# Layer 0 of a four-layer transformer stack: one program of sixteen half-batch rounds of four heads, in place of setup, two attentions and a feed-forward block

## The reference

```python
def cross_attention(q_in, kv_in, ...):           # H = 16 heads of K = 128
    qh = (q_in @ wq + bq).reshape(b, q_len, H, K)
    kh = (kv_in @ wk + bk).reshape(b, t, H, K)
    vh = (kv_in @ wv + bv).reshape(b, t, H, K)
    kh = concat([kh, bias_k]); vh = concat([vh, bias_v])      # a 257th key and value
    weights = softmax(einsum('bqhk,bthk->bhqt', qh, kh) / sqrt(K))
    return einsum('bhqt,bthk->bqhk', weights, vh).reshape(b, q_len, H * K) @ wo + bo

x = x + cross_attention(layer_norm(x, 1), ctx, weights 1)
x = x + cross_attention(layer_norm(x, 2), ctx, weights 2)
x = x + gelu(layer_norm(x, mlp) @ w_fc1 + b_fc1) @ w_fc2 + b_fc2     # inner width 1024
```

## Time and profile before

| | us |
|---|---|
| median of 3 runs (lowest, highest) | 1403.58 (1402.42, 1405.81) |
| the profiled execution | 1399.94 |
| its span, first to last instruction | 1398.2 |
| PE busy in the span | 1202.8 (86%) |
| DVE busy | 895.1 (64%) |
| ACT busy | 634.6 (45%) |
| POOL busy | 515.8 (37%) |

### The profile page before, as it was taken

The page is one execution under the profiler, slowest core; times in us unless marked ns, Lnnn a source line. Parts: engine busy times, 40 slices in busy tenths (PEclk is TensorE's granted clock), DMA queues, the critical chain, the costliest instruction groups (busy, mean ns, idle before and its releaser), DMA issues. The chain is left out here.

```text
span 1398.2 us, 22983 instructions
## 1 busy us (share of the span) xinstructions
PE 1202.8 (86%) x7772; PEld 942.0 (67%) x7772; DVE 895.1 (64%) x2170; ACT 634.6 (45%) x1427; POOL 515.8 (37%) x569
## 2 busy tenths in 40 slices
PE   4899999999689999999977759686576898889994
PEld 3698989998458899999955723332354676666664
DVE  5467667666546676666659243599564665767766
ACT  2356566655226565555534013100322574467770
POOL 2243344443214444344314012245001463167760
PEclk8999999999889999999998869798889899999998
DMA  6010000002000000000100020000002000000000
GB/s 199 16 32 16 30 30 30 30 8 83 0 31 31 31 30 30 23 30 15 61 1 0 9 67 1 0 1 0 0 24 61 1 2 2 0 1 2 2 2 31
DMA packets 32234, 33.56 MB, mean 24 GB/s; under 512 B 3833, under 2 KB 29730, under 8 KB 32162
## 3 DMA queue, kind: packets, MB, share of 16 engines
q1 hardware_dynamic: 31792, 31.73, 7.2%
q10 hardware_dynamic: 370, 0.91, 0.2%
HBM read 27.38 MB, written 1.05 MB: 20 GB/s over the span
## 5 line engine op out<-in xcount | busy, mean ns | idle before, releaser
L489 POOL TENSOR_TENSOR a_prob<-a_prob,a_inv_total 128x512 f32<-128x512 f32 x128 | 133.5, 1043 | 372.5 <-DVE a_inv_total L746 372.5
L1619 DVE CUSTOM_DVE_ANT_0 l_scores<-psum,mask 128x256 f32<-128x256 f32 x384 | 139.8, 421 | 70.8 <-PE psum L1572 70.8
L1629 POOL TENSOR_TENSOR l_scores<-l_scores,l_neg_max 128x512 f32<-128x512 f32 x144 | 147.8, 1041 | 100.7 <-DVE l_neg_max L1619 100.4
L656 ACT ACTIVATE a_prob<-psum,a_neg_max 128x257 f32<-128x257 f32 x256 | 119.3, 473 | 113.2 <-DVE a_neg_max L743 110.7
L1650 ACT ACTIVATE l_prob_T<-psum 128x512 f32<-128x512 f32 x192 | 108.8, 590 | 35.6 <-PE psum L1586 35.6
L1586 PE MATMUL psum<-ident,l_scores 128*128 128x128 f32 x768 | 117.0, 291 | 7.2 <-POOL l_scores L1629 4.1
L1586 PEld LDWEIGHTS psum<-ident,l_scores 128*128 128x128 f32 x768 | 85.5, 146 | 41.8 <-issue 19.2
L749 DVE TENSOR_TENSOR a_probT_lo<-psum,a_probT_hi 128x512 fp32r<-128x512 f32 x128 | 87.8, 686 | 22.2 <-ACT a_probT_hi L660 21.7
L598 PE MATMUL psum<-ident,a_prob 128*128 128x128 f32 x512 | 79.4, 278 | 11.0 <-POOL a_prob_bias L491 11.0
L743 DVE TENSOR_REDUCE a_neg_max<-psum 128x2 f32<-128x514 f32 x128 | 87.2, 681 | 0.0
L399 PE MATMUL psum<-a_k_hi,a_q_hi 128*128 128x258 f32 x256 | 76.9, 300 | 11.4 <-ACT a_prob L656 7.8
(11 more groups left out here) (336 smaller groups left out, 3342.7 us busy)
## 6 DMA issues: line engine op xcount, KB each, us to landing
wq_raw<-in_L_xattn_wq SPq DMA_DIRECT2D x16, 256.0 KB, 2.8
wk_raw<-in_L_xattn_wk SPq DMA_DIRECT2D x16, 256.0 KB, 2.8
wv_raw<-in_L_xattn_wv SPq DMA_DIRECT2D x16, 256.0 KB, 2.8
wo_raw<-in_L_xattn_wo SPq DMA_DIRECT2D x2, 2048.0 KB, 12.3
a_wo_pair<-wo_raw SPq DMA_DIRECT2D x16, 256.0 KB, 2.3
wo_raw<-in_L_xattn_w_fc SPq DMA_DIRECT2D x2, 1024.0 KB, 6.1
x_rows<-in_x SPq DMA_DIRECT2D x1, 1024.0 KB, 5.9
ctx_rows<-in_ctx SPq DMA_DIRECT2D x2, 512.0 KB, 9.6
```

Of the source, the lines that this page charges most:

```text
L489: pool.tensor_tensor(prob[:, u % 4, :, 0:S], prob[:, u % 4, :, 0:S], rtot[:, u % 4, :].unsqueeze(2).to_broadcast([P, 2, S]), ALU.mult)
L656: act.activation(prob[:, m % 4, q, 0:S + 1], s_bank(m)[:, q, 0:S + 1], ACT.Exp, bias=negm[:, m % 4, q:q + 1], accum_out=tot[:, m % 4, q:q ...
L1619: e = dve.tensor_tensor_reduce(sc[:, i % SC, q, :], s_bank(i)[:, q * S:(q + 1) * S], masks[:, b * NM + q % NM, :], 1.0, BIG, ALU.add, ALU. ...
L1629: pool.tensor_tensor(sc[:, i % SC, :, :], sc[:, i % SC, :, :], m[:, i % SC, :].unsqueeze(2).to_broadcast([P, 2, S]), ALU.subtract).then_in ...
```

## The change

Layer 0 becomes one block, `stage_layer0`, written out with no loop. Sixteen rounds follow each other through both attentions. A round is four heads over half the batches: rounds 0 to 3 do the first half (two batches) of attention 1, 4 to 7 its second half, 8 to 11 and 12 to 15 attention 2. There are eight units in a round as before. Four heads need twice the weights, so each matrix piece is 128x1024 and is loaded and cut in every round, each column of the weights twice per attention.

- In a round, V is four products of six 512-wide matmuls (before: twelve of 256), and O is two steps of 24 matmuls (before: four of 12). S, T, A, Q and K keep their number and size.
- `acc` has three banks (0, 1, 6), and the turned probabilities one (7).
- POOL cuts o, k and v in two halves of 128x512 each, k now behind norm 3 and norm 4.
- Layer norm of a half is spread over rounds 1 and 2 of the four before it is needed (X statistics, Y rows, L turning). B0, the products with the value biases, stands behind V3 in the eight rounds of a first half. P0 and one bias matmul per tile close each half.
- The first half of the feed-forward's first product (F0 to F7) takes the place of Q and K in round 15. Round 16 ends attention 2, and does the other half.
- Layer 1's weights go into the room of layer 0's raw weights, and SP loads them at layer 0's end. The normalised rows now lie in half of ctx, which is loaded again under layer 1's first layer norm.

```diff
-        acc = lambda n: ps[:, n % 2, :]
-        s_bank = lambda u: ps[:, 2 + 2 * (u % 2):4 + 2 * (u % 2), 0:KW]
-        t_bank = lambda u: ps[:, 6 + u % 2, :]
+    acc = lambda n: ps[:, (0, 1, 6)[n % 3], :]
+    s_bank = lambda g: ps[:, 2 + 2 * (g % 2):4 + 2 * (g % 2), 0:KW]
+    t_bank = lambda g: ps[:, 7, :].rearrange("p (k n) -> p k n", k=4)
...
+    base = ("S0 S1 O0 S2 O1 V0 T0 V1 S3 V2 T1 S4 V3 Q0 T2 S5 Q1 K0 T3 S6 K1 A0 T4 A1 "
+            "S7 T5 Q2 Q3 T6 K2 T7 K3 A2 A3").split()
+    last = ("S0 S1 O0 S2 O1 V0 T0 V1 S3 V2 T1 S4 V3 T2 S5 T3 S6 A0 T4 A1 "
+            "S7 F0 F1 T5 F2 F3 T6 F4 F5 T7 F6 F7 A2 A3").split()
...
+    out = {-1: "X0 X1 C0 C1 Y0 Y1 K0 K1 K2 K3 L0 L1 Q0 Q1 Q2 Q3".split()}
+    for i in range(LOOPS):
+        order = base if i < LOOPS - 1 else last
+        if i == 0:
+            order = [s for s in order if s[0] != 'O']
+            order = put(order, 'S1', 'C0', 'C1')
+        elif i % NQ == 0:
+            order = put(order, 'S0', 'P0')
+        if i // NQ % 2 == 0:
+            order = put(order, 'V3', 'B0')
+        if i % NQ == 1:
+            order = put(order, 'V1', 'X0')
+            order = put(order, 'V3', 'X1')
+            order = put(order, 'T3', 'Y0')
+            order = put(order, 'T4', 'Y1')
+        if i % NQ == 2:
+            order = put(order, 'V1', 'L0')
+            order = put(order, 'V2', 'L1')
+        out[i] = order
+    out[LOOPS] = "P0 O0 O1 X0 X1 Y0 Y1 G0 G1 L0 L1 F0 F1 F2 F3 F4 F5 F6 F7 G2 G3".split()
...
+                    norm(0)
+                    norm(1)
+                    if i:
+                        pool.wait_ge(acc_full, USE[i, 'O1'] + 1)
+                    cut_half('o', i, 0)
+                    norm(2)
+                    cut_half('o', i, 1)
+                    norm(3)
+                    pool.wait_ge(acc_full, USE[i - 1, 'K3'] + 1)
+                    cut_half('k', i + 1, 0)
+                    if i % NQ == 1:
+                        rstd_of(event_of(i))
+                    norm(4)
+                    cut_half('k', i + 1, 1)
+                    norm(5)
+                    if i % NQ == 2:
+                        h_low(event_of(i))
+                    pool.wait_ge(acc_full, USE[i, 'V3'] + 1)
+                    cut_half('v', i + 1, 0)
+                    norm(6)
+                    cut_half('v', i + 1, 1)
+                    norm(7)
...
+                        if k == 'K':
+                            if m == 0:
+                                pe.wait_ge(split['k'], i + 2)
...
+                        if k == 'T':
+                            g = i * U + m
+                            pe.wait_ge(s_norm, g + 1)
+                            if g >= T_BUFS:
+                                pe.wait_ge(t_free, g - T_BUFS + 1)
...
-    w = {n: sb(n, [P, NC, E1]) for n in L1_WEIGHTS}
+    place = [raw[n][:, :, i * E1:(i + 1) * E1] for n in 'qkv' for i in range(2)] + [raw['o'][:, 2 * i:2 * i + 2, :] for i in range(2)]
+    w = dict(zip(L1_WEIGHTS, place))
```

More of the change, by code:

```diff
@@ L86, in tiles_of @@
     return dram.rearrange("b (u p) d -> p (b u) d", p=P)
[L89 to L167, removed]
@@ new lines, in rows @@
+                def rows(dst, name, h, done):
+                    sp.dma_start(dst[:, h * HT:(h + 1) * HT, :], tiles_of(d[name])[:, h * HT:(h + 1) * HT, :]).then_inc(done, 16)
+                rows(chip.ctx, 'ctx_2048', 0, ld_ctx[0])
+                weights('k', 0)
+                rows(chip.x, 'x', 0, ld_x[0])
+                weights('q', 0)
+                weights('v', 0)
+                weights('o', 0)
+                rows(chip.ctx, 'ctx_2048', 1, ld_ctx[1])
+                rows(chip.x, 'x', 1, ld_x[1])
@@ L463, in _ @@
+                for j in range(1, LOOPS + 1):
+                    for n in 'qkvo':
+                        weights(n, j)
+                for n in 'qkvo':
+                    sp.wait_ge(split[n], LOOPS + 1)
                 prefetch(sp)
@@ L466, in _ @@
             def _(pool):
-                ones = one[:, 0:1].to_broadcast([P, NC, HW])
-                def cut(src, n, count, done):
-                    pool.tensor_tensor(whi[n][:, :, :], src, ones, ALU.mult).then_inc(rounded, 1)
-                    pool.wait_ge(rounded, count + 1)
-                    pool.tensor_tensor(wlo[n][:, :, :], src, whi[n][:, :, :].bitcast(F32), ALU.subtract).then_inc(done, 1)
+                pool.memset(chip.expo[:, :], -0.5)
+                pool.memset(chip.ident[:, :], 0.0).then_inc(ident_zero, 1)
@@ L480, in _ @@
[L480 to L494 removed]
+                cuts = [1]
@@ new lines, in cut @@
+                def cut(src, hi, lo, ends=None):
+                    pool.tensor_tensor(hi, src, one[:, 0:1].unsqueeze(2).to_broadcast([P] + list(src.shape[1:])) if len(src.shape) == 3
+                                       else one[:, 0:1].to_broadcast([P] + list(src.shape[1:])), ALU.mult).then_inc(rounded, 1)
+                    cuts[0] += 1
+                    pool.wait_ge(rounded, cuts[0])
+                    lo_ = pool.tensor_tensor(lo, src, hi.bitcast(F32), ALU.subtract)
+                    if ends is not None:
+                        lo_.then_inc(ends, 1)
@@ L850, in three @@
                     return pe.matmul(out, l_lo, r_hi, start=False, stop=last)
-                for n in range(NU):
-                    f = n // 2
-                    pe.wait_ge(w1_ok, f // 2 + 1)
-                    if n >= 4:
-                        pe.wait_ge(gelu, n - 3)
-                    for c in range(NC):
-                        mm = three(ps[:, n % 4, :], w1_hi[:, c, part(f)], w1_lo[:, c, part(f)], h_hi[:, c, half(n)], h_lo[:, c, half(n)], c == 0, c == NC - 1)
-                    mm.then_inc(full, 1)
```

954 lines of the change are left out of this document (476 added, 478 removed).

## The result

| | before | after |
|---|---|---|
| median of 4 runs each, us (lowest, highest) | 1404.69 (1402.42, 1410.11) | 1428.69 (1428.27, 1429.51) |
| after to before, 95% interval | | 1.0153 (1.0119 to 1.0187) |
| the profiled execution, us | 1399.94 | 1428.67 |

The change makes the kernel 24 us slower, or 1.5%. Forecast were 1442 us, with a range of 1395 to 1472 that holds the result, and a chance of 0.82 for slower. The profiled execution is 28.7 longer than that of before. I read it in the order of the prediction, with its rows of before beside it.

What follows compares the result with a forecast made beforehand. PE bounds the rounds, with openings only at the seams. Layer 0's start, rounds, waits, clock and end sum to 842 us against 798.2; with layer 1's seam +39, giving 1442 us, range 1395 to 1472.

Steps and rivals of the forecast that it cites:

- the clock: Behind PE's waits at K0 in rounds 0 to 14: half clock costs 1.9 us or 0.8 each, 24 us in all.
- round 15: F instead of Q and K, no K0, a cast and a remainder on DVE per F: 44 us.
- The place of the cut: In rounds, POOL cuts k behind norms 3 and 4, so PE waits at K0: 4.2 us, 2.2 with B0.
- B0's cover: In the eight rounds with B0, its 2.0 us are hidden by the wait for POOL and cost nothing.
- POOL in time: Rival: K0 finds k cut, its waits and the clock's cost fall away, B0 costs again: 1371 us; chance 0.14.
- The single bank: In each round T5 and T7 wait for the one bank of turned units: +0.8 us net, ends 0 and 2.
- X: Rounds 1, 5, 9, 13: a power on POOL ahead of norm 4 and row scalings on DVE, 2 us each.
- L: Rounds 2, 6, 10, 14: two steps ahead of the maximum norm 3 hangs on, on DVE and ACT, 2.4 us each.
- P0 with its bias matmuls: Rounds 4, 8, 12: costs 2 us each, 6 in all.
- The third rival: The clock stays low: every K0 wait gives 7 us at 1.2 GHz, 1469 us; chance 0.12.
- POOL late twice: Rival: norms 6 and 7 also late for T6 and T7, 2.4 us in 15 rounds, 1478 us; chance 0.10.
- the rule: Round 15: DVE instructions with both inputs in SBUF and POOL's cuts exclude each other, making the round 52 us.

Runs made afterwards that it cites:

- e4: Changed kernel with PSUM banks as before, two for products and two for turned units: 1420.94 us, ratio 1.0112.
- e2: Changed kernel with 12 to 40 unread matmuls a round filling PE's wait ahead of K0: 1407.58 us, ratio 1.0009.
- e3: Changed kernel with B0 behind K1 instead of behind V3, in the eight rounds that have it: 1445.36 us, ratio 1.0283.
- e1: Changed kernel with POOL's cut of k ahead of norm 3 and that of o behind it: 1359.75 us, ratio 0.9663.
- e5: Changed kernel with the edits of e1 and e4 together: 1360.94 us, ratio 0.969.

## Why the prediction was right, point by point

The terms of the sum for layer 0, and what the trace has in their place (a round goes from its first scores to the next round's):

| term | forecast | measured |
|---|---|---|
| first scores | 38 | 39.28 |
| round 0 | 42.6 and 0.8 of clock | 41.9 |
| rounds 1 to 14, with the clock | 661.5 | 649.6 |
| of rounds 0 to 14: waits at K0 | 47.0 | 49.9 |
| of them: turns and banks, net | 12 | 8 (e4) |
| of them: the clock | 24 | 21.2 (e2) |
| round 15 | 44 | 45.0 |
| behind round 15 | 55 | 52.8 |
| end of layer 0 | 842 | 828.7 |
| layer 1's seam | -4.7 | -4.5 |

**The place of the cut.** Right in kind and size: 4.2 without B0 and 2.2 with it were forecast, 4.2 and 2.6 came on average. B0's cover, claimed at 2.0 a round, was shown by e3. POOL in time was put at 1371 as a rival, by taking 63 and 24 away and 16 back. e1, which makes it so, gives 1359.75. Its gain from the changed kernel, 69 us, is near the 71 of that sum; the rest of the difference is the 13 us by which the whole sum is too long. (The 14 loop ends named with this rival are 12: rounds 1 to 6 of two attentions.)

**The single bank.** +0.8 net a round, 12 in all, against 8 by e4. That it was a term at all depends on the late k: with k in time, e5 gains nothing over e1. The prediction had T5 and T7 alone waiting. In rounds 6 and 14 T2 waits too, for 1.47 and 1.49 us:

```profile
332.90 0.63 PE L566 MATMUL psum<-ident,a_prob 128*128 128x128 f32 x4 [1.47 <-DVE a_probT_lo L733]
```

**Where the sum is too long.** e2 has the changed kernel's rounds at full clock, so it helps to take apart the 13.3 us by which the forecast of rounds 0 to 14 is too long (704.9 with the clock, 691.6 measured). From first scores to first scores, each round of one kind within 0.1 us of the others:

| rounds | forecast without clock | e2 |
|---|---|---|
| 0 | 42.6 | 40.4 |
| plain (3, 7, 11) | 43.9 | 43.4 |
| X (1, 5, 9, 13) | 45.9 | 44.6 |
| L (2, 6, 10, 14) | 46.3 | 45.3 |
| P (4, 8, 12) | 45.9 | 46.7 |
| sum of 0 to 14 | 680.8 | 670.4 |
| the clock on top | 24 | 691.6 less 670.4, 21.2 |

The plain round is 0.5 too long in the forecast and round 0 is 2.2 too long. The layer-norm steps were mis-sized: X adds 1.2 us to a plain round and not 2, L 1.9 and not 2.4. P0 with its bias matmuls adds 3.3 and not 2. In X rounds the wait for k is 1.1 longer than in plain rounds (5.15 and 5.10 against 4.05, 3.13 and 3.10 against 1.95 and 2.01): that is POOL's power ahead of norm 4, as it was counted, and nearly all of what X costs. The row scalings on DVE, counted beside it, added next to nothing. In L rounds the wait for k is 3.00 and 2.97 with B0, 1.0 more than in plain rounds; without B0 it is 3.37, but PE has stood 1.47 at T2 just before (row above), 4.8 together against 4.05. The rest of L's 1.9 fits its two turnings on PE, 0.60 us each in their rows. The misses partly cancel, which is luck: P, round 15 and the first scores came out 4.7 us above their terms together, and the other terms of layer 0, with its end, 18 below. The seams ahead of round 0 and behind round 15 were checked by their totals alone. The last 3.6 us of the forecast, added since the profiled execution before lay that far under its median, did not come either: the changed kernel's lies at its median (1428.67 and 1428.69).

The clock is right in its total. By round it is the changed kernel less e2: nothing in rounds 2, 3, 9 and 14; 1.4 to 1.6 us in rounds 0, 4, 7, 8, 10, 11 and 12; 2.1 to 2.7 in rounds 1, 5, 6 and 13. The prediction had ordered it by the length of the wait, 1.9 or 0.8, and that order does not hold. Stretches of 3.40 us from K0 on, in rounds 2, 6, 8 and 9 (columns as in rows 1):

```profile
154.72:158.12 3.40, 3.40 (x20) 2.95 (x21) 0.85 (x2) 1.73 (x6) 0.00 (x0) 1.00 0.55 152
339.01:342.41 3.40, 3.40 (x10) 2.71 (x11) 0.00 (x0) 0.46 (x1) 0.00 (x0) 0.50 0.52 154
...
433.35:436.75 3.40, 3.40 (x11) 2.71 (x11) 0.16 (x1) 0.59 (x2) 0.00 (x0) 0.52 0.49 154
479.50:482.90 3.40, 3.40 (x20) 2.96 (x21) 0.85 (x2) 1.74 (x6) 0.00 (x0) 1.00 0.53 154
```

Behind waits of 3.00, 3.10 and 3.37 us (rounds 2, 9, 14) the clock stayed at 2.4 GHz, and 20 matmuls started where 10 or 11 start at 1.2. Behind the 1.95 of round 8 it fell to half, and behind another 3.37, that of round 6, it was half and then 0.66 in the next 3.4 us. What tells these apart the runs do not show. The third rival, a long slow stretch behind every wait, did not come.

**POOL late twice.** Refuted. In round 7 it idles for 4.44 us ahead of norm 5, and no turn waits for a norm in the changed kernel.

**Round 15 and the remainders.** By the row of 1.02 us I gave 44, by the rule 52 would have come; it is 45.0. The casts and remainders there, in order of time beside POOL's cuts of v that end at 762.55:

```profile
760.02 1.40 DVE L814 TENSOR_TENSOR a_q_lo<-a_ln_full,a_q_hi 128x512 fp32r<-128x512 f32 x1
...
761.95 0.89 DVE L812 CAST a_q_hi<-a_ln_full 128x512 fp32r<-128x512 f32 x1
762.87 0.69 DVE L814 TENSOR_TENSOR a_q_lo<-a_ln_full,a_q_hi 128x512 fp32r<-128x512 f32 x1
```

One of the eight remainders took 1.40 beside the cuts, and one cast 0.89 where the other seven took 0.42 to 0.46. The other seven remainders took 0.69, since POOL had no more to cut by then. The Trainium skill's rule (SBUF — State Buffer, Who interferes with whom), by which I had worked out the 52, was therefore not refuted by this round: what was wrong was to count a cut beside every remainder.

## What to carry to other kernels

When a job is doubled, look first at where it stands in its engine's queue and who comes to wait for it, and only then at how busy that engine is: here two places in POOL's order made the difference between 1.5% slower and 3.4% faster, with the same busy time. Put what another engine wants first (k) ahead of whatever waits for data, and what is wanted late (o) behind it. A wait in a dense stretch of matmuls costs more than its length, here 21 us on top of 50. And the price of a small thing depends on the larger one beside it: B0 is free only while k is late, and the single bank cost 8 us then and nothing afterwards.
